# Shared node windows for four or two groups of edges, and VectorE's wait for products placed ahead of its one-hot rows

## The reference

```python
# layer 0
edge_input = concatenate([x[dst], x[src], edge_attr, u[batch[dst]]], axis=1)
aggregated = segment_sum(relu(edge_input @ W1.T + b1), dst)
x = layernorm(x + relu(concatenate([x, aggregated, u[batch]], axis=1) @ W2.T + b2))
# layer 1
h = relu(concatenate([x[src], x[dst], edge_attr], axis=-1) @ msg_w1 + msg_b1)
summed = segment_sum(h @ msg_w2 + msg_b2, dst);  counts = segment_sum(ones, dst)
x = layernorm(x + (relu(concatenate([x, summed / max(counts, 1)]) @ upd_w1 + upd_b1) @ upd_w2 + upd_b2))
```

## Time and profile before

| | |
|---|---|
| median of 3 runs | 4737.94 us (4737.09 to 4750.91) |
| profiled execution | 4797.05 us, of it span 4795.3 us |
| mean granted TensorE clock | 0.541 of 2.4 GHz |
| PE busy | 3389.9 us, 71%, 16937 matmuls |
| POOL busy | 2958.2 us, 62% |
| DVE busy | 1628.8 us, 34% |
| ACT busy | 593.8 us, 12% |
| chain that ended last | PE 62%, issue 25%, unknown queue 9%, DVE 2% |

### The profile page before, as it was taken

One profiled execution on the slowest core, in us unless ns is written; L12 is line 12 of the kernel. 1 busy time (PEld: TensorE's weight loads), 2 busy tenths in 40 slices (PEclk: granted clock), 3 DMA queues, 4 the chain that ended last, 5 costly groups with the idle time before them and its releaser, 6 DMA issues.

```text
span 4795.3 us, 47299 instructions
## 1 busy us (share of the span) xinstructions
PE 3389.9 (71%) x16937; PEld 3156.9 (66%) x16937; DVE 1628.8 (34%) x4012; ACT 593.8 (12%) x1017; POOL 2958.2 (62%) x3156
## 2 busy tenths in 40 slices
PE   5777777777777677777746766677677777666767
PEld 4676666666676667767646666666666666666666
DVE  4333333333333333333423333333333223223223
ACT  1110111111111111111111111111111111111111
POOL 5666666656666666666556666666666666666663
PEclk7555555555555555555665555555555555555555
DMA  6443333433334334334423333334334334433432
GB/s 206 123 141 115 114 115 104 118 113 119 114 119 120 117 107 123 120 114 120 127 90 116 115 116 116 117 118 127 115 112 120 117 117 119 118 118 113 122 118 87
DMA packets 291344, 567.98 MB, mean 118 GB/s; under 512 B 166870, under 2 KB 186817, under 8 KB 266140
## 3 DMA queue, kind: packets, MB, share of 16 engines
q1 hardware_dynamic: 168120, 339.88, 21.7%
q0 software_dynamic: 100032, 205.00, 16.4%
q10 hardware_dynamic: 22948, 20.00, 1.3%
HBM read 545.15 MB, written 19.45 MB: 118 GB/s over the span
## 4 chain that ended last, share of the span: by engine, by line
PE 62%; issue 25%; another core or an unknown queue 9%; DVE 2%; DMA 1%; SPq 0%; ACT 0%; DVEq 0%; ACTq 0%
PE bank L1052 26%; PE bank L1066 24%; PE bank L1057 7%; DMA BIG<-in_dstR 1%; DVE BIG L1316 1%; PE bank L997 1%; PE bank L959 1%; PE bank L991 1%; PE bank L972 0%; PE bank L1002 0%; PE bank L1015 0%; PE bank L1037 0%; PE bank L1028 0%; DMA BIG<-tabP 0%
## 5 line engine op out<-in xcount | busy, mean ns | idle before, releaser
L283 POOL DMA_INDIRECT Qr<-tabQ,srcE x3106 | 2936.2, 945 | 1785.1 <-issue 879.6
L1066 PE MATMUL bank<-BIG 128*128 128x42 f32 x6252 | 1433.1, 386 | 645.5 <-issue 642.9
L1066 PEld LDWEIGHTS bank<-BIG 128*128 128x128 f32 x6252 | 1395.8, 312 | 687.9 <-issue 685.0
L1052 PE MATMUL bank<-wall,BIG 128*128 128x128 f32 x6252 | 1590.3, 420 | 319.0 <-issue 306.7
L1052 PEld LDWEIGHTS bank<-wall,BIG 128*128 128x128 f32 x6252 | 1380.7, 315 | 361.7 <-issue 360.8
L1316 DVE TENSOR_TENSOR BIG<-bank,Qr 128x512 f32<-128x512 f32 (+1 forms) x782 | 536.1, 686 | 1572.0 <-remote 1295.0
L1211 ACT ACTIVATE BIG<-BIG 128x512 f32<-128x512 f32 (+1 forms) x782 | 492.2, 629 | 3820.5 <-DVE BIG L1316 3136.1
L1057 PE MATMUL bank<-BIG 126*128 126x128 bf16 x3126 | 515.4, 299 | 307.6 <-issue 290.9
L1057 PEld LDWEIGHTS bank<-BIG 126*128 126x128 bf16 x3126 | 377.9, 140 | 390.8 <-issue 323.6
L1334 DVE TENSOR_TENSOR AC<-AC,bank 128x84 f32 (+1 forms) x782 | 167.8, 215 | 1326.2 <-remote 946.6
L1226 DVE TENSOR_TENSOR BIG<-bank,BIG 126x512 bf16<-126x512 f32 x782 | 533.9, 683 | 149.6 <-DMA BIG<-in_dstR 81.0
(11 more groups left out here) (132 smaller groups left out, 605.7 us busy)
## 6 DMA issues: line engine op xcount, KB each, us to landing
BIG<-in_eaT SPq DMA_DIRECT2D x194, 1024.0 KB
BIG<-in_dstR SPq DMA_DIRECT2D x194, 504.0 KB
Qr<-tabQ,srcE POOLq DMA_INDIRECT x3106
BIG<-tabP SPq DMA_DIRECT2D x782, 31.5 KB
tabP<-BIG ACTq DMA_DIRECT2D x22, 384.0 KB
tabQ<-BIG ACTq DMA_DIRECT2D x17, 256.0 KB
X<-in_xN SPq DMA_DIRECT2D x1, 3136.0 KB
out<-BIG ACTq DMA_DIRECT2D x11, 256.0 KB
```

What stands on the lines that cost most here:

```text
L283: e.indirect_dma_start(Q[0:p, i % R_Q, j, :], None, tabQ[l][:, :], bass.IndirectOffsetOnAxis(ap=srcE[0:p, g, j:j + 1], axis=0)).then_inc(f ...
L1052: e.matmul(bank[i % R_C][:, j * D:(j + 1) * D], f_eaT[:, k % R_EA, (g % LQ * J + j) * P:(g % LQ * J + j + 1) * P], wc[l], start=(j == 0), ...
L1066: last = e.matmul(bank[4 + i % 2][:, 0:W], M[:, i % R_M, j, :], S[:, i % R_S, j, :], start=(j == 0), stop=(j == n - 1))
```

## The change

The groups of a layer are put into windows: the first 104 groups in 26 windows of four, the next 100 in 50 windows of two, the other 187 alone, so 263 windows in place of 391. All groups of a window use the node span that begins with the first destination of the window's first group (`base` on the host). Then:

- the load of 42 node rows into `PB` is issued once per window, and TensorE waits for it at the window's first group;
- L1066's sums of a window's groups collect in one bank (`start` at the first group, `stop` at the last), and the counting matmul, the sum into `S16` (now over 16, 8 or 4 tiles) and the addition to `AC` are done once, at the window's last group; `v_ag` counts windows;
- waits on `v_ag` stay only where a window ends; `S` has 8 slots in place of 6 (`hot`), so that a window's four lie side by side; `READY` is rounded up to the end of a window (115, 161, 197 become 116, 162, 198);
- on VectorE the wait for the last group's products (`v_C`) moves from just ahead of the add to the head of the step, ahead of `rows_hot(i + 1)`.

```diff
-R_EA, R_PB, R_BC, R_Q, R_ST, R_S, R_M, R_PT, R_U = 2, 4, 2, 10, 3, 6, 3, 4, 2
+R_EA, R_PB, R_BC, R_Q, R_ST, R_S, R_M, R_PT, R_U = 2, 4, 2, 10, 3, 8, 3, 4, 2
...
+FOURS, PAIRS = 26, 50
+WIN = [(4 * k, 4) for k in range(FOURS)] + [(4 * FOURS + 2 * k, 2) for k in range(PAIRS)]
+WIN += [(g, 1) for g in range(4 * FOURS + 2 * PAIRS, NG)]
+NWIN = len(WIN)
+WIN_OF = [w for w, (_, n) in enumerate(WIN) for _ in range(n)]
...
+def window(i):
+    l, g = divmod(i, NG)
+    return l * NWIN + WIN_OF[g]
...
 (fast_sync)
-                    if i >= R_PB:
-                        e.wait_ge(v_C, i - R_PB + 1)
-                    e.dma_start(PB[0:K, i % R_PB, :], tabP[l][bass.ds(at[g % LQ], W), :].rearrange("w (h d) -> (w h) d", d=D)).then_inc(f_pb[i % R_PB], 16)
+                    if first_of(i):
+                        w = window(i)
+                        if w >= R_PB:
+                            e.wait_ge(v_C, window_end(w - R_PB))
+                        e.dma_start(PB[0:K, w % R_PB, :], tabP[l][bass.ds(at[g % LQ if len(at) > 1 else 0], W), :].rearrange("w (h d) -> (w h) d", d=D)).then_inc(f_pb[w % R_PB], 16)
...
 (fast_tensor)
-                        e.wait_ge(f_pb[i % R_PB], 16 * (i // R_PB + 1))
+                        w = window(i)
+                        if first_of(i):
+                            e.wait_ge(f_pb[w % R_PB], 16 * (w // R_PB + 1))
...
-                            if j == tiles(g) - 1 and i >= 4:
-                                e.wait_ge(v_ag, i - 3)
+                            if j == tiles(g) - 1 and i >= 4 and windows_done(i - 3) > windows_done(i - 4):
+                                e.wait_ge(v_ag, windows_done(i - 3))
...
-                            last = e.matmul(bank[4 + i % 2][:, 0:W], M[:, i % R_M, j, :], S[:, i % R_S, j, :], start=(j == 0), stop=(j == n - 1))
-                        if l == 0:
-                            last = e.matmul(bank[4 + i % 2][:, W:2 * W], onesb[:, :], S16[:, i % R_S, :], start=True, stop=True)
+                            last = e.matmul(sums[:, 0:W], M[:, i % R_M, j, :], S[:, hot(i), j, :],
+                                            start=(j == 0 and first_of(i)), stop=(j == n - 1 and last_of(i)))
+                        if l == 0 and last_of(i):
+                            last = e.matmul(sums[:, W:2 * W], onesb[:, :], S16[:, w % R_S, :], start=True, stop=True)
...
 (fast_vector)
+                        if g:
+                            e.wait_ge(v_C, i)
                         if i + 1 < 2 * NG:
                             rows_hot(e, i + 1)
-                        if g > 3:
-                            e.wait_ge(v_ag, i - 3)
+                        if g > 3 and windows_done(i - 3) > windows_done(i - 4):
+                            e.wait_ge(v_ag, windows_done(i - 3))
...
-                        if l == 0:
+                        if l == 0 and last_of(i):
...
-                                e.tensor_reduce(S16[:, i % R_S, :], S[:, i % R_S, :, :].rearrange("p j w -> p w j"), AX, ALU.add).then_inc(v_cn, 1)
-                        e.wait_ge(v_C, i + 1)
+                                e.tensor_reduce(S16[:, w % R_S, :], S[:, h:hot(i) + 1, :, :].rearrange("p r j w -> p w (r j)"), AX, ALU.add).then_inc(v_cn, 1)
+                        if g == NG:
+                            e.wait_ge(v_C, i + 1)
                         e.wait_ge(f_q[i % R_Q], q_count(i))
...
-                    if 3 <= g < NG + 3:
+                    if 3 <= g < NG + 3 and last_of(l * NG + g - 3):
```

More of the change, by code:

```diff
@@ L50, with first_of, last_of, window_end @@
 NU = len(UN)
+FOURS, PAIRS = 26, 50
[3 more added lines that the diff above has]
+WIN_OF = [w for w, (_, n) in enumerate(WIN) for _ in range(n)]
+def first_of(i):
+    l, g = divmod(i, NG)
+    return g == WIN[WIN_OF[g]][0]
+def last_of(i):
+    l, g = divmod(i, NG)
+    return g == sum(WIN[WIN_OF[g]]) - 1
+def window(i):
+    l, g = divmod(i, NG)
+    return l * NWIN + WIN_OF[g]
+def window_end(w):
+    return w // NWIN * NG + sum(WIN[w % NWIN])
+def windows_done(i):
+    return window(i) if i < 2 * NG else 2 * NWIN
 def edges_below(node):
@@ L886, in build, with hot @@
         p_c, p_hi, p_r, p_mid, p_lo = p1s
+        def hot(i):
+            return i % NG % R_S
         def quad_done(k):
@@ L969, in y0 @@
                     y0_features(u)
-                e.wait_ge(v_ag, READY[u])
+                e.wait_ge(v_ag, windows_done(READY[u]))
                 for k in range(n):
@@ L1054, in fast_tensor @@
                         for j in range(tiles(g)):
-                            if j == tiles(g) - 1 and i >= 4:
-                                e.wait_ge(v_ag, i - 3)
-                            last = e.matmul(bank[i % R_C][:, j * D:(j + 1) * D], ST[0:K, i % R_ST, j * P:(j + 1) * P], PB[0:K, i % R_PB, :], start=False, stop=(j == tiles(g) - 1))
+                            if j == tiles(g) - 1 and i >= 4 and windows_done(i - 3) > windows_done(i - 4):
+                                e.wait_ge(v_ag, windows_done(i - 3))
+                            last = e.matmul(bank[i % R_C][:, j * D:(j + 1) * D], ST[0:K, i % R_ST, j * P:(j + 1) * P], PB[0:K, w % R_PB, :], start=False, stop=(j == tiles(g) - 1))
                         last.then_inc(v_C, 1)
@@ L1230, in mean @@
                 w, b = UN[u][1] * P, UN[u][0] * P
-                e.wait_ge(v_ag, NG + READY[u])
+                e.wait_ge(v_ag, windows_done(NG + READY[u]))
                 if u:
@@ L1292, in fast_vector @@
             e.wait_ge(s_ac, 3)
+            loaded = None
             for l in range(2):
@@ L1299, in fast_vector @@
                             rows_hot(e, 0)
+                        if g:
+                            e.wait_ge(v_C, i)
                         if i + 1 < 2 * NG:
                             rows_hot(e, i + 1)
-                        if g > 3:
-                            e.wait_ge(v_ag, i - 3)
+                        if g > 3 and windows_done(i - 3) > windows_done(i - 4):
+                            e.wait_ge(v_ag, windows_done(i - 3))
                         rel = relE[:, g, :].unsqueeze(2).broadcast_to([P, J, W])
                         io = bank[6][:, NGP:NGP + W].unsqueeze(1).broadcast_to([P, J, W])
-                        e.tensor_tensor(S[:, i % R_S, :, :], io, rel, ALU.is_equal).then_inc(v_s, 1)
+                        e.tensor_tensor(S[:, hot(i), :, :], io, rel, ALU.is_equal).then_inc(v_s, 1)
                     if 1 <= g < NG + 1:
                         i = l * NG + g - 1
-                        if l == 0:
+                        if l == 0 and last_of(i):
+                            w = window(i)
+                            h = hot(i) + 1 - WIN[w][1]
                             e.wait_ge(v_s, i + 1)
-                            with nc.allow_low_precision(reason="a sum of four zeros or ones"):
-                                e.tensor_reduce(S16[:, i % R_S, :], S[:, i % R_S, :, :].rearrange("p j w -> p w j"), AX, ALU.add).then_inc(v_cn, 1)
-                        e.wait_ge(v_C, i + 1)
+                            with nc.allow_low_precision(reason="a sum of at most sixteen zeros or ones"):
+                                e.tensor_reduce(S16[:, w % R_S, :], S[:, h:hot(i) + 1, :, :].rearrange("p r j w -> p w (r j)"), AX, ALU.add).then_inc(v_cn, 1)
+                        if g == NG:
+                            e.wait_ge(v_C, i + 1)
                         e.wait_ge(f_q[i % R_Q], q_count(i))
@@ L1323, in fast_vector @@
                         last_terms(e, g // 16)
[L1324 removed]
+                    if 3 <= g < NG + 3 and last_of(l * NG + g - 3):
                         i = l * NG + g - 3
[L1326 to L1327 removed]
+                        w = window(i)
+                        if loaded != i // NG * NQ + (g - 3) // LQ:
+                            loaded = i // NG * NQ + (g - 3) // LQ
+                            at = bases(mybir.EngineType.DVE, (g - 3) // LQ * LQ)
                         e.wait_ge(v_A, i + 1)
[L1329 to L1331 removed]
+                        if w and (w == NWIN or g >= NG):
+                            e.wait_ge(v_ag, w)
+                        if w == NWIN:
                             e.wait_ge(s_mz, NU)
[L1333 to L1334 removed]
+                        acc = AC[:, 0:ctl, bass.ds(at[(g - 3) % LQ if len(at) > 1 else 0], W)]
+                        e.tensor_tensor(acc, acc, bank[4 + w % 2][:, 0:ctl * W].rearrange("p (t w) -> p t w", w=W),
                                         ALU.add).then_inc(v_ag, 1)
@@ L1491, in laid_out @@
         "dstR": dstp.astype(_np.int16).reshape(1, EP),
-        "base": dstp.astype(_np.int32)[::GE].reshape(1, NGP),
+        "base": dstp.astype(_np.int32)[[GE * (WIN[WIN_OF[g]][0] if g < NG else g) for g in range(NGP)]].reshape(1, NGP),
         "wall": _np.concatenate(parts, axis=1),
```

8 lines of the change are left out of this document (5 added, 3 removed).

## The result

The changed kernel takes 4857.49 us (median of 4 runs, 4855.39 to 4878.53) against 4743.27 (4737.09 to 4750.91) for the kernel before in the same comparison: ratio **1.0236**, 95% interval 1.0212 to 1.0259, some 114 us slower. The forecast was 4827, the range 4700 to 4895. The profiled execution of the changed kernel (4855.39 us) lies at its median, while that of the kernel before (4797.05) lies 54 us above its own; so the two traces differ by 58 us where the medians differ by 114, and I read kinds and counts from the traces and sizes from the ratios.

The account below looks back on a forecast made before the run. The prediction took a fixed gather time plus GpSimd's stops, waiting for VectorE's add, as the bound. Its terms, 160 - 51 - 8 - 12 = +89 us, on the median 4737.94 gave 4827 us, range 4700 to 4895.

Parts of the forecast that it names:

- The bound: Whole kernel: a fixed gather time plus the sum of GpSimd's stops, together 4691 of the 4795 us.
- The moved wait: VectorE ahead of the add: rows and columns lengthen 162 stops, 0.84 us in layer 1, 1.19 in layer 0, +160 us.
- What comes back: GpSimd's stops: longer stops give TensorE more undisturbed time, so 11 of 218 stops fewer, -51 us.
- rival B: At the stops: longer clear time lets a fifth group through and returns in full; within 14 us of 4738; chance 0.13.
- The windows: Merged work per window: -8 us for counting matmuls, -12 for additions to the totals, 0 for node-row loads.
- The step on the additions: VectorE's additions to the totals: 256 fewer; 25 of 42 stops that ended with one shorten by 0.5 us, -12 us.
- the matmuls: TensorE in layer 0: 128 counting matmuls fewer, by the rule of stops -8 us.
- The signs: In the new profile: GpSimd's add wait 960 us, layer 1 gap 4.9, slightly fewer stops, rows and columns before add.
- A: TensorE's instructions set the pace and stops are only a symptom: 36 to 154 us less, 4702 to 4584; chance 0.17.
- C's first half: GpSimd's stops follow the feature loads' rhythm, staying above 210; nothing comes back: 148 us, 4886; chance 0.15 for both halves.
- C's second half: TensorE also waits for later one-hot rows, 0.60 us at 218 stops: 131 us more, 5017; chance 0.15 for both halves.
- D: At the windows: one is wider than 42 nodes, so the general program runs, far outside any range; chance 0.01.

Follow-up runs that it names:

- the dose: Changed kernel plus an unread VectorE reduction of 672 numbers between the wait and the one-hot rows: 4988.45 us, ratio 1.0358 against the kernel before.
- the halfway wait: Changed kernel with the wait put behind the one-hot rows and ahead of the columns: 4826.27 us, ratio 1.0041 against the kernel before.
- the cut add: Changed kernel with the wait back ahead of the add, whose first tile alone releases the first gather: 4734.96 us, ratio 0.9853; again 4681.9 us, 0.9857.

## Why the prediction was right

**The bound** held. In every trace of the table the gathers' time stays, the rest is 21 to 60 us, and what differs between the kernels is the stops.

**The moved wait** was forecast at 160 - 51 = +109 us and measured +89 [73, 105] by itself, below the forecast. The length of the usual stop was right: in layer 1 the median of 4.04 us became 4.98 in the changed kernel against the 4.9 forecast, with rows and columns of 0.85 as priced. Single stops are less regular; the one at 3019.52 waited 3.71 us for its release. As a rule that lag did not grow: where VectorE stood at the head of its step in layer 1, the median lag from the last gather to the release was 2.97 us, against 3.08 ahead of the add before. In layer 0 I forecast 1.19 us more; the median grew by 0.95.

**What comes back** was forecast as 11 of 218 stops, 5%, from a longer stop letting more of TensorE's work through. With the moved wait alone the stops over 0.8 us only fell from 213 to 209; in the three traces of the changed kernel they were 200, 206 and 208. More came back in another way: not every stop grew. With the change of layer aside the mean stop went from 4.07 to 4.60 us with the moved wait alone, 0.53 more, where the forecast had 160 / 218 = 0.73. In all some 70 us of the 160 came back (160 - 89), where I had 51, and only a part of it by fewer stops. Of the stretches between two stops of over 2 us (one of 13 groups in every trace aside), 7 served five groups or more before, 38 with the moved wait alone, 18 with the windows alone, and 84, 56 and 84 in the changed kernel. So a fifth group does get through, most with both edits together, as rival B had it; but it paid back only a part.

**The windows**, -8 for matmuls, -12 for additions and 0 for loads, made -20; measured -29 [-40, -18]. How it splits among them is open. The step on the additions holds in part: the stops over 2 us in which VectorE's longest wait was at the addition to the totals fell, with the windows alone, from 47 to 30 in layer 0, but rose from 1 to 7 in layer 1, 11 fewer where I had 25. The moved wait shifts them too: alone it has 15 and 30, the changed kernel 19 and 26. On the matmuls the queue depth of 64 that the Trainium skill gives for TensorE (Advanced Engine Details and Errata, Engine Queue Depths) led to an estimate of 19 us beside my 8; no run here tells the two apart.

**The sum** is where the size was off, and that it read +89, as the moved wait alone does, is chance. The parts measured alone give 89 - 29 = +60 us, some 41 to 79 with their intervals; the whole gave 1.017, 1.0221 and 1.0236, some 82, 105 and 112 us by the ratios. On the chip of 1.017 the interval (65 to 98) overlaps that of the sum; the parts were measured on another chip. In the sums of stops the parts do add: 994 + 879 - 903 = 970 us, against 956, 976 and 954 in the traces of the changed kernel. Whether the parts strengthen each other or chips differ is open, since no chip ran all three.

**The signs.** Rows, columns, add after a release and gaps of 4.9 us came as named, and so did a few stops fewer. TensorE's halting still ended some 3 us after a last gather. GpSimd's row for the add did not rise to 960; its idle time did rise, but in rows of other names, so that sign was badly chosen. The issue total, which was to stay, rose for the same reason.

**The rivals.** A (a symptom, faster) fell: the dose, the halfway wait and the cut add move the time with the path to the add alone, TensorE's work unchanged. B fell by size. C's first half fell by size too, 148 us against 82 to 112; its count, above 210 stops, was missed only narrowly, with 200 to 208. C's second half fell by TensorE's 0.8 us of waiting for the one-hot rows. D did not occur, as the merged loads and matmuls show.

## What to carry to other kernels

Where a producer stands still until one instruction on another engine has started, what is queued between that engine's own release and that instruction lengthens the stops, however idle the engine is on average (here some 90 of 160 us were left when a part had come back); put waits directly ahead of the instruction that needs them, with independent work ahead of the wait. Then look at the other end: cutting the releasing instruction so that its first part frees the first slot gave 1.5% here, some 0.6% of it the windows'. Count a stalled queue's gaps from its own starts and ends, since the row that names the releaser can stay the same while the gaps grow.

## What the runs showed of the hardware

- **The same kernel takes 4743 to 4817 us on some chips and 3947 on one.** There, in the traces of the windows alone with and without the counting matmuls, TensorE doesn't halt while GpSimd gathers, though the gathers are as long (945 ns each in both). The granted clock was 0.562 there and 0.541 in the first profile; that alone can't be it, since the clear stretches run at the same pace (one group's first product takes 2.06 us in both, at 1001.23 there and 516.13 here). What makes TensorE halt on the others is open.
- **On a chip that halts, half the gathers took away nearly all of the halting:** the "issue" gaps ahead of the first product fell from 306.7 us in the first profile to 30.7, and the time fell by 1,730 us of 4,801, with a mean granted clock of 0.620.
- **VectorE's next instruction starts before the last one ends:** in the stop at 675.89 the columns start at 676.50, 0.08 us before the rows' recorded end at 676.58; so the price of an instruction in a chain is read from start to start.
